# Gated delta stage: the state kept through the update banks by identity products, and the first solved value not copied

## The chip, the cores and the metric

The kernel runs on one core of one Trainium2 chip. The metric is the device time of one execution in microseconds, the median of several runs. The engines are called by their names: TensorE (PE in the profile; PEld is its weight load), VectorE (DVE), ScalarE (ACT), GpSimd (POOL) and SyncE (SP, which issues the DMAs).

## The reference, cut to what matters

The program computes four layers on an activation of 4 x 512 tokens with 128 features; each half layer is followed by a residual sum and a layer norm. The change is in the first of the eight stages, a gated delta rule with 16 heads of 64:

```python
q = silu(dwconv(x @ Wq.T)); k = silu(dwconv(x @ Wk.T)) * 64 ** -0.5; v = silu(dwconv(x @ Wv.T))
a = sigmoid(x @ Wa.T + ba); beta = sigmoid(x @ Wb.T + bb)
def step(S, inp):
    qt, kt, vt, at, bt = inp
    err = einsum('bhij,bhj->bhi', S, kt) - vt
    S = at[..., None] * S - bt[..., None, None] * (err[..., None] * kt[:, :, None, :])
    return S, einsum('bhij,bhj->bhi', S, qt)
S, o = lax.scan(step, S0, xs)          # over the 512 tokens
o = headnorm(o) * ln_w + ln_b; o = o * sigmoid(x @ Wg.T); return o @ Wo.T
```

All arithmetic is in float32. The state S is 64 x 64 for each of 4 x 16 heads, decayed by rows with `a` at each token.

## The kernel before, in words

`delta_attention` (lines 2219 to 2875) cuts the 512 tokens into 16 chunks of 32 (`NC`, `CP`); one pass of the loop works on one chunk n, in two halves e = 0, 1 of 16 tokens, and each half in two blocks u = 0, 1 of 8 tokens. Each engine has its own program, written out by hand; they meet in semaphores, and each engine takes its instructions strictly in order.

In a half, VectorE does this (`one_pass` of the vector block): `steps(n, e, 0)` solves the triangular system of the first 8 tokens, one token after the other, with a product (line 2788) and a sum (2792) for each token over all earlier ones, and a decay of the values so far (2779); `middle` decays what goes over to the second block, decays the state by the whole half (2754, into `ST`) and adds what TensorE computed across the blocks; `steps(n, e, 1)` solves the second block. Its last value releases the transpose into `W` (2784), called the turn in what follows. Then `end` transposes the outputs (2805) and the decays and values of the next chunk into `Y` (2691, 2692), waits for the updates of the state and adds them to the decayed state in four adds of 128x512 (2812), one for each PSUM bank of `UPDATES`. `prepare` (scan at 2697, product at 2700) builds the prefix products of the decays for the next chunk; `norm`, for e = 0 only, is the head norm of the chunk before (2816, 2818); `begin` opens the next half: the transpose of the start products out of PSUM into `Y` (2732) and the inputs of its first block (2722 to 2725). `begin` waits for `laid`, since it overwrites `Y`, from which ScalarE copies, and for `y`, the start products.

TensorE, `boundary(n, e)`: waits for `W`, transposes it in four products with the identity (2437), two for each half of `WT`, waits for ScalarE's copies of them into `WT` (2609), runs 64 small matmuls of 32x64 weights (2448), which put K^T W for the four row groups r into four banks, and then, as each quarter of `ST` is ready, the start products of the next half (2421). Behind that, in its queue, are the projections of the next chunk (2360, 2363), the head norm's sums (`centre` 2463, `variance` 2474), `out` (2482), and for e = 1 the products of the next keys (2374, ahead of the boundary). In e = 0 the boundary stands behind a wait for ScalarE's evacuation of `vN` (line 2555) and in e = 1 behind the products of keys, which wait for the last evacuation of the projections.

ScalarE, around a boundary: the two copies into `WT` (2609), `lay_out` for the next chunk (decays out of `Y` into `aT` 2615, two small copies 2618, 16 copies of values into `bv` 2622, each of them counted by `laid`), `scale_decays` (16 copies into `FB`, 2629, after VectorE's scan), then evacuations.

SyncE's queue holds `spread`: it takes `whole`, from `prepare`, to DRAM and broadcasts it back into `Abc`, which the next decay of the state (2754) reads.

The functions that the diff touches follow.

Of the kernel before, what the change touches and what calls it, by code (L numbers as in the profile page):

```python
# [15 lines left out]
ALU = mybir.AluOpType  # L16
ACT = mybir.ActivationFunctionType
AXX = mybir.AxisListType.X

P = 128  # L20
# [2198 lines left out]
def delta_attention(c):  # L2219
# [17 lines left out]
    GR, GP = 4, NP // 4  # L2237
    UPDATES = (6, 7, 0, 1)
    BEGUN = 7
    GC = 2 * SB * CP + SB  # L2240
# [5 lines left out]
    with ExitStack() as ctx:  # L2246
# [61 lines left out]
        later_ps = ps[:, 4:6, :].rearrange("p h (a n x) -> p h a n x", n=GR, x=XC // 2)  # L2308
        centred_ps = ps[:, 4:6, :].rearrange("p k x -> p (k x)")
        yield []  # L2310
        block = c.block(ctx)
# [38 lines left out]
        def _(eng):  # L2350
# [74 lines left out]
            def boundary(n, e):  # L2425
                j4 = 8 * n + 4 * e

                def next_start(r):
                    eng.wait_ge(s["state"], j4 + max(r + 1, 2 * e))
                    eng.sem_inc(c.past, 1)  # L2430
                    start(1 - e, r)

                eng.wait_ge(s["w"], 4 * n + 2 * e + 2)
                eng.sem_inc(c.past, 1)
                for half in range(2):
                    for g in (2 * half, 2 * half + 1):
                        mm = eng.transpose(ps[:, half, (g % 2) * P:(g % 2 + 1) * P],
                                           W[:, g * GP:(g + 1) * GP, :], c.ident[:, :])
                    mm.then_inc(s["t"], 1)
                eng.wait_ge(s["wc"], 6 * n + 3 * e + 3)  # L2440
                eng.sem_inc(c.past, 1)
                for g in range(GR):
                    for k in range(2):
                        for h in range(2):
                            for r in range(GR):
                                rows, cols = slice(32 * r, 32 * r + 32), slice(DK * h, DK * h + DK)
                                at = (2 * g + k) * DK
                                mm = eng.matmul(ps[cols, UPDATES[r], at:at + DK], KT[rows, e, k, g, cols], WT[rows, g, DK * (h ^ k):DK * (h ^ k) + DK], start=True, stop=True)
                                if (g, k, h) == (GR - 1, 1, 1):
                                    mm.then_inc(s["upd"], 1)  # L2450
                for r in range(GR):
                    next_start(r)
                if e == 1:
                    eng.wait_ge(s["gt"], 2 * n + 3)
                    eng.sem_inc(c.past, 1)
                    later_products(n + 1)
# [82 lines left out]
        def _(eng):  # L2539
# [66 lines left out]
            def boundary(n, e):  # L2606
                for half in range(2):
                    eng.wait_ge(s["t"], 6 * n + 3 * e + half + 2)
                    eng.activation(WT[:, 2 * half:2 * half + 2, :], ps[:, half, 0:2 * P].rearrange("p (g x) -> p g x", x=P), ACT.Copy)\
                       .then_inc(s["wc"], 1)  # L2610

            def lay_out(m, e):
                at = 2 * m + e + 1
                eng.wait_ge(s["transposed"], 3 * at - 2)
                eng.activation(aT[:, e, :, :, 1:].rearrange("p i u t -> p u t i"), decays[:, :, :].rearrange("p (u t) i -> p u t i", t=SB), ACT.Copy)\
                   .then_inc(s["laid"], 1)
                for sign in range(2):
                    eng.activation(beta_now[:, sign, :], half_of(beta, m, e), ACT.Copy, scale=1.0 - 2.0 * sign).then_inc(s["laid"], 1)
                eng.wait_ge(s["transposed"], 3 * at - 1)
                eng.wait_ge(s["laid"], 4 * at - 9)  # L2620
                for t in range(CH):
                    ins = eng.activation(bv[:, e, :, t], values[:, t, :], ACT.Copy, scale=beta_now[:, 0, t:t + 1])
                ins.then_inc(s["laid"], 1)
# [12 lines left out]
            def one_pass(n, first):  # L2636
# [9 lines left out]
                evacuate(n + 1, 2, AV)  # L2646
                boundary(n, 0)
                lay_out(n + 1, 0)
                scale_decays(n + 1, 0)
# [5 lines left out]
                evacuate(n + 1, 6, PROJ)  # L2655
                boundary(n, 1)
                lay_out(n + 1, 1)
                later_products(n + 1)
# [18 lines left out]
        def _(eng):  # L2677
            LINKS = 1 + 3 * SB - 1

# [62 lines left out]
            def middle(n, e):  # L2742
# [8 lines left out]
                eng.tensor_tensor(rest, rest, half[:, e, :].unsqueeze(1).to_broadcast([P, CH, I]), ALU.mult).then_inc(s["begun"], 1)  # L2751
                eng.wait_ge(s["abc"], 2 * 16 * j + 32)
                state = ST[:, :, :].rearrange("p n (s i) -> p n s i", i=I)
                eng.tensor_tensor(state, state, Abc[:, e, :, :, :].rearrange("p s n i -> p n s i"), ALU.mult).then_inc(s["decayed"], 1)
# [7 lines left out]
            def steps(n, e, u):  # L2762
# [12 lines left out]
                settled()  # L2775
                link(eng.tensor_copy(mine[:, :, 0], XP[:, 0, :, SB]))
                for t in range(SB):
                    if t:
                        link(eng.tensor_tensor(mine[:, :, 0:t], mine[:, :, 0:t], aT[:, e, :, u, t + 1].unsqueeze(2).to_broadcast([P, I, t]), ALU.mult))  # L2779
# [6 lines left out]
                    x, keys, seen = 2 * (at + t) + 1, slice(at, at + t + 1), mine[:, :, 0:t + 1]  # L2786
                    if t < SB - 1:
                        link(eng.tensor_tensor(XP[:, :, :, SB - t:], seen.unsqueeze(1).to_broadcast([P, 2, I, t + 1]),  # L2788
                                               G[:, x:x + 2, keys][:, ::-1, :].unsqueeze(2).to_broadcast([P, 2, I, t + 1]), ALU.mult))
                        settled()  # L2790
                        to = first + t + 1
# [9 lines left out]
            def end(n, e, first):  # L2801
                j = 2 * n + e
                if e == 0 and not first:
                    eng.wait_ge(s["centred"], n)
                eng.transpose(O[:, e * CH:(e + 1) * CH, :], OT.rearrange("p i t -> p t i")).then_inc(s["o"], 1)
                turn_values(n + 1, e)
                eng.wait_ge(s["decayed"], j + 1)
                quarters = ST[:, :, :].rearrange("p (g r k) i -> p r g (k i)", r=GR, k=2)
                for r in range(GR):
                    eng.wait_ge(s["upd"], 4 * j + r + 1)  # L2810
                    mine = quarters[:, r, :, :]
                    eng.tensor_tensor(mine, mine, ps[:, UPDATES[r], :].rearrange("p (g x) -> p g x", g=GR), ALU.add).then_inc(s["state"], 1)  # L2812

# [11 lines left out]
            def one_pass(n, first):  # L2825
# [3 lines left out]
                end(n, 0, first)  # L2829
                prepare(n + 1, 0)  # L2830
                if not first:
                    norm(n - 1)
                begin(n, 1)
                steps(n, 1, 0)
# [194 lines left out]
```

## Time and profile before

| | before |
|---|---|
| time, median of 3 runs (lowest, highest) | 2884.49 us (2883.37, 2885.67) |
| the profiled execution's own time | 2877.2 us |
| its span in the trace | 2875.3 us |
| TensorE busy over the span | 2342.6 us (81%) |
| VectorE busy | 2143.5 us (75%) |
| ScalarE busy | 1553.6 us (54%) |
| mean granted TensorE clock | 0.881 of 2.4 GHz |

The span is what the hardware profiler saw from the first to the last instruction. Busy time is the sum over an engine's instructions. A row of the timeline gives the begin and the length of a group of equal instructions in a row, the engine, the line, the operation, what it writes and reads, their number, and in brackets how long the engine stood idle before it and which instruction ended that. Matmuls in float32 appear as two records each. A mean share over the whole span mixes stages: the delta stage is the first 1310 us.

### The profile page before, as it was taken

What the parts mean: (1) busy time and instruction counts of PE and PEld (TensorE: products, weight loads), DVE (VectorE), ACT (ScalarE), POOL (GpSimd) and SP (SyncE); (2) the same over time, 40 slices, a digit from 0 to 9 for tenths busy, and PEclk for the clock granted to TensorE, in tenths of its full rate; (3) what the DMA queues carried; (4) which work ended last, traced back from release to release, by engine and by line L of the source; (5) the groups of instructions that cost most, each with busy time, mean ns of one, the idle gap of its engine ahead of it and who ended that gap; (6) DMA issues with size and microseconds to landing.
All of it is one profiled execution on the core that took longest, in us unless ns stands there. A gap on an engine that the chain in (4) does not pass through costs nothing. (4 is left out here: it accounts for less than half of the span.)

```text
span 2875.3 us, 63093 instructions
## 1 busy us (share of the span) xinstructions
PE 2342.6 (81%) x25365; PEld 1619.3 (56%) x25365; DVE 2143.5 (75%) x4003; ACT 1553.6 (54%) x3983; POOL 264.0 (9%) x278
## 2 busy tenths in 40 slices
PE   6777777777777777777984999999887876999677
PEld 5667667666677667673432666666542322332376
DVE  6999999999999999993123777787626765886465
ACT  3555556666555555655233777777631113667344
POOL 0000000000000000000011101100002431110342
PEclk9888787887887887888996999999998997999888
DMA  5110111110111110102006998899410003221421
GB/s 183 32 31 18 31 31 32 32 32 21 27 31 32 32 31 18 31 17 70 0 11 178 233 250 227 227 248 235 103 37 0 0 0 105 55 82 24 170 70 64
DMA packets 205722, 219.42 MB, mean 76 GB/s; under 512 B 32966, under 2 KB 191446, under 8 KB 199990
## 3 DMA queue, kind: packets, MB, share of 16 engines
q1 hardware_dynamic: 203033, 210.44, 28.1%
q0 software_dynamic: 2400, 4.95, 0.5%
q8 instruction: 203, 3.33, 0.5%
q14 instruction: 86, 0.70, 0.1%
HBM read 137.96 MB, written 79.79 MB: 76 GB/s over the span
## 5 line engine op out<-in xcount | busy, mean ns | idle before, releaser
L2792 DVE TENSOR_REDUCE dl_ZO<-dl_XP 128x64 f32<-128x128 f32 (+6 forms) x448 | 219.8, 491 | 15.4
L2788 DVE TENSOR_TENSOR dl_XP<-dl_ZO,dl_G 128x64 f32<-128x64 f32 (+6 forms) x448 | 194.7, 435 | 15.4
L1973 ACT ACTIVATE da_AB<-ps 128x384 f32<-128x384 f32 x256 | 124.7, 491 | 140.8 <-PE ps L1834 137.2
L2126 DVE TENSOR_TENSOR ps<-ps,da_window 128x192 f32<-128x192 f32 (+1 forms) x256 | 101.3, 396 | 116.8 <-PE ps L1857 112.6
L1453 DVE TENSOR_REDUCE ra_top<-ps 128x1 f32<-128x512 f32 x256 | 159.5, 681 | 36.9 <-PE ps L1219 35.9
L1983 ACT ACTIVATE da_E<-ps,da_top 128x512 f32<-128x512 f32 x256 | 176.2, 688 | 17.5 <-DVE da_top L2129 17.0
L2129 DVE TENSOR_REDUCE da_top<-ps 128x1 f32<-128x512 f32 x256 | 177.0, 691 | 8.8
L1864 PE MATMUL ps<-ident,da_E 128*128 128x128 f32 x1024 | 169.1, 288 | 1.3 <-ACT da_E L1983 1.3
L1353 ACT ACTIVATE ra_PT<-ps 128x512 f32<-128x512 f32 x256 | 136.2, 600 | 61.7 <-PE ps L1250 61.4
L2421 PE MATMUL ps<-dl_kqN,dl_ST 64*64 64x32 f32 x4096 | 114.2, 282 | 42.2 <-DVE dl_ST L2812 36.9
L2363 PE MATMUL ps<-X,dl_taps_q 128*128 128x128 f32 x1088 | 148.3, 304 | 0.0
L2363 PEld LDWEIGHTS ps<-X,dl_taps_q 128*128 128x128 f32 x1088 | 145.2, 219 | 1.8
L1584 POOL MEMSET da_K<- 32x4096 f32 x2 | 7.0, 3505 | 1494.8 <-POOLq L178 1494.7
L2363 PE MATMUL ps<-X,dl_taps_k 128*128 128x128 f32 x1088 | 143.6, 297 | 0.4 <-issue 0.4
L2363 PEld LDWEIGHTS ps<-X,dl_taps_k 128*128 128x128 f32 x1088 | 140.4, 213 | 1.5 <-issue 0.5
L1864 PEld LDWEIGHTS ps<-ident,da_E 128*128 128x128 f32 x1024 | 108.4, 141 | 50.3 <-issue 39.7
L2421 PEld LDWEIGHTS ps<-dl_kqN,dl_ST 64*64 64x64 f32 x4096 | 109.3, 209 | 48.1 <-issue 47.9
L2363 PEld LDWEIGHTS ps<-X,dl_taps_v 128*128 128x128 f32 x1088 | 127.0, 195 | 13.6 <-issue 8.5
L2629 ACT ACTIVATE dl_FB<-dl_F,dl_beta_now 128x32 f32<-128x32 f32 x512 | 126.8, 351 | 9.6 <-DVE dl_F L2697 9.6
L2363 PE MATMUL ps<-X,dl_taps_v 128*128 128x128 f32 x1088 | 127.2, 277 | 4.7 <-DVE dl_taps_v L2853 3.8
L2779 DVE TENSOR_TENSOR dl_ZO<-dl_ZO,dl_aT 128x32 f32<-128x32 f32 (+6 forms) x448 | 128.2, 286 | 0.0
L1219 PE MATMUL ps<-ra_KS,ra_QS 128*128 128x512 bf16 x256 | 104.5, 413 | 12.8 <-DMA ra_KS<-ra_parts 10.2
(404 smaller groups left out, 5726.8 us busy)
## 6 DMA issues: line engine op xcount, KB each, us to landing
da_bands<-da_AB SPq DMA_DIRECT2D x128, 384.0 KB, 3.8
dl_Abc<-dl_ends SPq DMA_DIRECT2D x64, 512.0 KB, 6.3
da_window<-da_bands SPq DMA_DIRECT2D x128, 192.0 KB, 4.4
da_across<-da_bands SPq DMA_DIRECT2D x128, 192.0 KB, 4.5
da_parts<-da_split SPq DMA_DIRECT2D x64, 96.0 KB, 3.4
ra_parts<-ra_split SPq DMA_DIRECT2D x16, 384.0 KB, 3.7
rf_We<-in_rf_We SPq DMA_DIRECT2D x1, 4608.0 KB, 22.9
da_K<-da_parts SPq DMA_DIRECT2D x16, 256.0 KB
```

The lines of the kernel that those rows point to most:

```text
L1353: eng.activation(PT[:, k % 2, h, :], ps[:, tscore_bank(UNITS * m + v), :], ACT.Exp).then_inc(s["exps"], 1)
L1453: eng.tensor_reduce(top[:, m % 2, u:u + 1], ps[:, score_bank(UNITS * m + u), :], AXX, ALU.max, negate=True).then_inc(s["maxima"], 1)
L1864: mm = eng.transpose(ps[:, 2 + U % 2, k * P:(k + 1) * P], E[:, U % 2, k * P:(k + 1) * P], c.ident[:, :])
L1973: eng.activation(AB[:, j % STAGES, h, :, :], ps[:, band_bank(v), 0:2 * BAND].rearrange("p (k x) -> p k x", k=2), ACT.Copy)\
L1983: eng.activation(E[:, U % 2, :], ps[:, score_bank(U), :], ACT.Exp, bias=top[:, u:u + 1], accum_out=total[:, m % 2, u:u + 1]).then_inc(s["e ...
L2129: eng.tensor_reduce(top[:, u:u + 1], bank, AXX, ALU.max, negate=True).then_inc(s["maxima"], 1)
L2363: mm = eng.matmul(out, taps[w][:, tap, cols], columns_of(c.X, m, tap), start=tap == 0, stop=tap == TAPS - 1)
L2421: mm = eng.matmul(starts_ps[e][DK * (h ^ w):DK * (h ^ w) + DK, w, pair // 2, :], ST[rows, pair, :], kqN[rows, pair, e * CH:(e + 1) * CH, : ...
L2629: ins = eng.activation(FB[:, e, :, t // SB, t % SB], F[:, e, :, t // SB, t % SB], ACT.Copy, scale=beta_now[:, 1, t:t + 1])
L2779: link(eng.tensor_tensor(mine[:, :, 0:t], mine[:, :, 0:t], aT[:, e, :, u, t + 1].unsqueeze(2).to_broadcast([P, I, t]), ALU.mult))
L2788: link(eng.tensor_tensor(XP[:, :, :, SB - t:], seen.unsqueeze(1).to_broadcast([P, 2, I, t + 1]), G[:, x:x + 2, keys][:, ::-1, :].unsqueeze ...
L2792: link(eng.tensor_reduce(ZO[:, to:to + 1 + (2 * I - 1) * CH:CH].rearrange("p (k i) -> p k i", k=2), XP[:, :, :, SB - 1 - t:], AXX, ALU.add))
```

## The change

The state is no longer added up on VectorE. TensorE puts the decayed state into the four update banks by a product with the identity for each (`kept`, 512 columns, start=True), the update matmuls add to it there (start=False), and ScalarE copies each bank back into `ST` (`keep_state`), between the copy of the decays and the rest of `lay_out`, which is cut in two for that. `EARLY` says how many of the four identity products stand ahead of the wait for `W`: four for e = 0 and three for e = 1, where the transposes of `W` take bank 1, the fourth update bank; there the fourth identity product and the sixteen updates of r = 3 come last. For e = 0 the transposes of `W` go to banks 2 and 3, for e = 1 both halves to bank 1, so that ScalarE's first copy there waits for both. The next decay of the state on VectorE waits for ScalarE's copies.

In `steps` the first solved value, which was copied out of `XP` and decayed at t = 1, is written already decayed; the product of t = 0 reads it from `XP`, and no decay is issued at t = 1. In `one_pass` of VectorE `norm` and `prepare` of e = 0 change places.

```diff
+    TURNED = ((2, 3), (1, 1))
+    EARLY = (4, 3)
...
+        quarters = ST[:, :, :].rearrange("p (g r k) i -> p r g (k i)", r=GR, k=2)
...
+                def kept(r):
+                    eng.matmul(ps[:, UPDATES[r], :], c.ident[:, :], quarters[:, r, :, :], start=True, stop=False)
+
+                def update(g, k, h, r):
+                    rows, cols = slice(32 * r, 32 * r + 32), slice(DK * h, DK * h + DK)
+                    at = (2 * g + k) * DK
+                    last = (g, k, h) == (GR - 1, 1, 1)
+                    mm = eng.matmul(ps[cols, UPDATES[r], at:at + DK], KT[rows, e, k, g, cols],
+                                    WT[rows, g, DK * (h ^ k):DK * (h ^ k) + DK], start=False, stop=(g, k) == (GR - 1, 1))
+                    if last:
+                        mm.then_inc(s["upd"], 1)
+
+                early = EARLY[e]
+                eng.wait_ge(s["decayed"], 2 * n + e + 1)
+                for r in range(early):
+                    kept(r)
                 eng.wait_ge(s["w"], 4 * n + 2 * e + 2)
...
-                        mm = eng.transpose(ps[:, half, (g % 2) * P:(g % 2 + 1) * P],
-                                           W[:, g * GP:(g + 1) * GP, :], c.ident[:, :])
+                        mm = eng.transpose(ps[:, TURNED[e][half], g * P:(g + 1) * P], W[:, g * GP:(g + 1) * GP, :], c.ident[:, :])
...
-                for g in range(GR):
-                    for k in range(2):
-                        for h in range(2):
-                            for r in range(GR):
...
+                for g, k, h, r in itertools.product(range(GR), range(2), range(2), range(early)):
+                    update(g, k, h, r)
+                for r in range(early, GR):
+                    kept(r)
+                    for g, k, h in itertools.product(range(GR), range(2), range(2)):
+                        update(g, k, h, r)
...
-                    eng.wait_ge(s["t"], 6 * n + 3 * e + half + 2)
+                    eng.wait_ge(s["t"], 6 * n + 3 * e + (3 if e else half + 2))
...
+            def keep_state(n, e):
+                for r in range(GR):
+                    eng.wait_ge(s["upd"], 8 * n + 4 * e + r + 1)
+                    eng.activation(quarters[:, r, :, :], ps[:, UPDATES[r], :].rearrange("p (g x) -> p g x", g=GR), ACT.Copy).then_inc(s["state"], 1)
...
                 boundary(n, 0)
+                lay_decays(n + 1, 0)
+                keep_state(n, 0)
                 lay_out(n + 1, 0)
...
+                if j:
+                    eng.wait_ge(s["state"], 4 * j)
...
-                link(eng.tensor_copy(mine[:, :, 0], XP[:, 0, :, SB]))
+                link(eng.tensor_tensor(mine[:, :, 0], XP[:, 0, :, SB], aT[:, e, :, u, 2], ALU.mult))
                 for t in range(SB):
-                    if t:
+                    if t > 1:
...
+                    if t == 0:
+                        link(eng.tensor_tensor(XP[:, ::-1, :, SB:], XP[:, 0, :, SB:].unsqueeze(1).to_broadcast([P, 2, I, 1]),
+                                               G[:, x:x + 2, keys].unsqueeze(2).to_broadcast([P, 2, I, 1]), ALU.mult))
+                    elif t < SB - 1:
...
-                eng.wait_ge(s["decayed"], j + 1)
-                quarters = ST[:, :, :].rearrange("p (g r k) i -> p r g (k i)", r=GR, k=2)
-                for r in range(GR):
-                    eng.wait_ge(s["upd"], 4 * j + r + 1)
-                    mine = quarters[:, r, :, :]
-                    eng.tensor_tensor(mine, mine, ps[:, UPDATES[r], :].rearrange("p (g x) -> p g x", g=GR), ALU.add).then_inc(s["state"], 1)
...
-                prepare(n + 1, 0)
                 if not first:
                     norm(n - 1)
+                prepare(n + 1, 0)
```

## Rows read from the trace of the kernel before

**Rows 1.** Windows: length, busy time of each engine (instructions), clock, DMA share, GB/s.
```profile
0.00:1310.00 1310.00, 1000.99 (x17026) 895.15 (x17027) 1205.92 (x2381) 761.00 (x2254) 0.20 (x4) 0.83 0.15 36
```

**Rows 2.** Waits of VectorE, 80 to 1300 us: total, times, longest.
```profile
DVE dl_ST L2812 <- PE ps L2448: 25.0, 28, 2.2
```

**Rows 3.** Timeline of VectorE around three boundaries: start, length, engine, line, operation.
```profile
625.03 1.05 DVE L2784 STREAM_TRANSPOSE dl_W<-dl_ZO 128x512 f32<-128x512 f32 x1
628.45 0.67 DVE L2692 STREAM_TRANSPOSE dl_Y<-dl_vN 128x512 f32<-128x512 f32 x1
630.16 2.48 DVE L2812 TENSOR_TENSOR dl_ST<-dl_ST,ps 128x512 f32<-128x512 f32 x4 [1.03 <-PE ps L2448]
...
636.59 1.24 DVE L2732 STREAM_TRANSPOSE dl_Y<-ps 128x1024 f32<-128x1024 f32 x1
...
664.65 1.07 DVE L2784 STREAM_TRANSPOSE dl_W<-dl_ZO 128x512 f32<-128x512 f32 x1
...
669.26 2.48 DVE L2812 TENSOR_TENSOR dl_ST<-dl_ST,ps 128x512 f32<-128x512 f32 x4 [0.51 <-PE ps L2448]
...
676.07 1.25 DVE L2732 STREAM_TRANSPOSE dl_Y<-ps 128x1024 f32<-128x1024 f32 x1
...
704.18 1.05 DVE L2784 STREAM_TRANSPOSE dl_W<-dl_ZO 128x512 f32<-128x512 f32 x1
```

**Rows 4.** Timeline of ScalarE, in the same passes.
```profile
606.06 1.13 ACT L2582 ACTIVATE dl_Q<-ps 128x512 f32<-128x512 f32 x2
...
621.71 1.26 ACT L2555 ACTIVATE dl_vN<-ps,dl_vec 128x128 f32<-128x128 f32 x4 [0.92 <-PE ps L2363]
626.94 0.81 ACT L2609 ACTIVATE dl_WT<-ps 128x256 f32<-128x256 f32 x2 [3.97 <-PE ps L2437]
...
629.51 0.27 ACT L2618 ACTIVATE dl_beta_now<-dl_beta 128x16 f32<-128x16 f32 x2
629.88 3.53 ACT L2622 ACTIVATE dl_bv<-dl_Y,dl_beta_now 128x32 f32<-128x32 f32 x16
...
702.77 1.26 ACT L2555 ACTIVATE dl_vN<-ps,dl_vec 128x128 f32<-128x128 f32 x4 [0.93 <-PE ps L2363]
```

**Rows 5.** Timeline of VectorE, begin of one block of `steps`.
```profile
600.24 0.20 DVE L2776 COPY dl_ZO<-dl_XP 128x32 f32<-128x32 f32 x1
...
600.78 0.30 DVE L2792 TENSOR_REDUCE dl_ZO<-dl_XP 128x64 f32<-128x128 f32 x1
...
601.25 0.31 DVE L2788 TENSOR_TENSOR dl_XP<-dl_ZO,dl_G 128x128 f32<-128x128 f32 x1
```

**Rows 6.** Timeline of TensorE, pieces of several passes.
```profile
190.60 2.10 PE L2374 MATMUL ps<-dl_kqN,dl_kkN 64*64 64x64 f32 x128 [1.45 <-ACT dl_kqN L2555]
193.98 0.63 PE L2437 MATMUL ps<-ident,dl_W 128*128 128x128 f32 x4 [1.29 <-issue]
...
195.23 1.50 PE L2448 MATMUL ps<-dl_WT,dl_KT 32*64 32x64 f32 x118 [0.62 <-ACT dl_WT L2609]
...
236.38 1.84 PE L2448 MATMUL ps<-dl_WT,dl_KT 32*64 32x64 f32 x128 [0.62 <-ACT dl_WT L2609]
...
600.00 1.95 PE L2463 MATMUL ps<-dl_O,dl_sums 128*128 128x512 f32 x4 [0.29 <-ACT dl_GX L2569]
...
601.79 1.95 PE L2467 MATMUL ps<-X,dl_Wg 128*128 128x128 f32 x16
...
611.93 0.68 PE L2407 MATMUL ps<-dl_GX,dl_WT 64*64 64x64 f32 x16
...
627.90 2.18 PE L2448 MATMUL ps<-dl_WT,dl_KT 32*64 32x64 f32 x128 [0.56 <-ACT dl_WT L2609]
...
663.84 2.10 PE L2374 MATMUL ps<-dl_kqN,dl_kkN 64*64 64x64 f32 x128 [1.45 <-ACT dl_kqN L2555]
```

**Rows 7.** Windows of 2 us, columns as in rows 1.
```profile
600.00:602.00 2.00, 2.00 (x6) 1.04 (x7) 1.83 (x8) 2.00 (x10) 0.00 (x0) 1.00 0.15 42
...
628.00:630.00 2.00, 2.00 (x128) 1.94 (x128) 1.12 (x2) 1.34 (x4) 0.00 (x0) 0.53 0.03 8
```

**Rows 8.** Groups by line, delta stage: busy, mean ns, idle before, releaser.
```profile
L2609 ACT ACTIVATE dl_WT<-ps 128x256 f32<-128x256 f32 x64 | 22.6, 383 | 102.5 <-PE ps L2437 101.9
```

More of the change, by code:

```diff
@@ L2441, in boundary @@
                 eng.sem_inc(c.past, 1)
-                for g in range(GR):
-                    for k in range(2):
-                        for h in range(2):
-                            for r in range(GR):
[L2446 to L2450, printed above, removed]
+                for g, k, h, r in itertools.product(range(GR), range(2), range(2), range(early)):
[4 more added lines that the diff above has]
+                        update(g, k, h, r)
                 for r in range(GR):
@@ L2607, in boundary, with lay_decays @@
                 for half in range(2):
-                    eng.wait_ge(s["t"], 6 * n + 3 * e + half + 2)
-                    eng.activation(WT[:, 2 * half:2 * half + 2, :], ps[:, half, 0:2 * P].rearrange("p (g x) -> p g x", x=P), ACT.Copy)\
-                       .then_inc(s["wc"], 1)
-            def lay_out(m, e):
+                    eng.wait_ge(s["t"], 6 * n + 3 * e + (3 if e else half + 2))
+                    eng.activation(WT[:, 2 * half:2 * half + 2, :], ps[:, TURNED[e][half], half * 2 * P:(half + 1) * 2 * P].rearrange("p (g x) -> p g x", x=P),
+                                   ACT.Copy).then_inc(s["wc"], 1)
+            def lay_decays(m, e):
                 at = 2 * m + e + 1
@@ L2616, in lay_out @@
                    .then_inc(s["laid"], 1)
+            def keep_state(n, e):
+                for r in range(GR):
+                    eng.wait_ge(s["upd"], 8 * n + 4 * e + r + 1)
+                    eng.activation(quarters[:, r, :, :], ps[:, UPDATES[r], :].rearrange("p (g x) -> p g x", g=GR), ACT.Copy).then_inc(s["state"], 1)
+            def lay_out(m, e):
+                at = 2 * m + e + 1
                 for sign in range(2):
@@ L2656, in one_pass @@
                 boundary(n, 1)
+                lay_decays(n + 1, 1)
+                keep_state(n, 1)
                 lay_out(n + 1, 1)
@@ L2677, in _ @@
         def _(eng):
-            LINKS = 1 + 3 * SB - 1
+            LINKS = 3 * SB - 1
             def gate_keys(m):
@@ L2786, in steps @@
                     x, keys, seen = 2 * (at + t) + 1, slice(at, at + t + 1), mine[:, :, 0:t + 1]
-                    if t < SB - 1:
+                    if t == 0:
+                        link(eng.tensor_tensor(XP[:, ::-1, :, SB:], XP[:, 0, :, SB:].unsqueeze(1).to_broadcast([P, 2, I, 1]),
+                                               G[:, x:x + 2, keys].unsqueeze(2).to_broadcast([P, 2, I, 1]), ALU.mult))
+                    elif t < SB - 1:
                         link(eng.tensor_tensor(XP[:, :, :, SB - t:], seen.unsqueeze(1).to_broadcast([P, 2, I, t + 1]),
                                                G[:, x:x + 2, keys][:, ::-1, :].unsqueeze(2).to_broadcast([P, 2, I, t + 1]), ALU.mult))
+                    if t < SB - 1:
                         settled()
@@ L2801, in end @@
             def end(n, e, first):
-                j = 2 * n + e
                 if e == 0 and not first:
```

## The prediction, written before the changed kernel was run

> **What bounds the kernel now.** I read the windows first, then the waits of VectorE, then the timelines of VectorE, ScalarE and TensorE around the boundaries between half passes. In the delta stage, which takes the first 1310 us, VectorE is busy 92% of the time and TensorE 76% [rows 1]: VectorE sets the pace. Its waits say where it stops: 25.0 us in 28 stops in front of the state adds of line 2812, [rows 2]; no other wait of it comes near that. So the stage ends when VectorE's queue ends, and what VectorE drops is gained only as far as the next instruction that waits for another engine doesn't come to wait longer. That instruction is the opening transpose of a half pass (line 2732, in `begin`): it overwrites `Y`, and so waits for `laid`, the last of the 16 `bv` copies on ScalarE, and for `y`, the four start products on TensorE. In the trace it waits for neither.
>
> I count time from the turn, the end of the transpose into W (line 2784). In the e = 0 boundary the turn is at 625.03 + 1.05 = 626.08, the state adds begin at 630.16 (+4.08) and the opening transpose at 636.59 (+10.51). In the e = 1 boundary the turn is at 665.72, the adds begin at 669.26 (+3.54), the opening transpose at 676.07 (+10.35) [rows 3]. These two distances are what the change moves. ScalarE has spare time behind its part: the `bv` row ends at 629.88 + 3.53 = 633.41 [rows 4], +7.33, which is 3.2 us before VectorE asks.
>
> **VectorE alone.** Each boundary loses four adds, 2.48 us, and its stop in front of them (630.16 less 628.45 + 0.67 = 1.04 us, [rows 3]). The second edit is in `steps`: the copy becomes a product of the same 32 elements, and the separate product at t = 1 goes. Before, copy to second XP product is 601.25 - 600.24 = 1.01 us. After, the reduce that begins at 600.78 has no product beside it and the XP product waits for its end: 0.54 us from the copy, 0.30 of reduce, 0.04 for the release, 0.88. That is 0.13 us for each of 64 `steps`, not the 0.25 of the deleted row, since it ran under the end of the reduce [rows 5]. Per pass 0.52 us. Norm in front of prepare puts VectorE work ahead of a wait for `aT`, which ScalarE has ready by then; it costs nothing. The transfers of `dl_ends` on SP's queue, which prepare releases, come later by norm's two instructions and sooner by the adds and the stop, 3.5 us, so not later than now.
>
> **TensorE: the 128 identity products are not free.** An identity product of 512 columns is not in the trace, but `centre` has two of that form: they begin at 600.00 and the next row at 601.79, 0.895 us each [rows 6], at a granted clock of 1.00 [rows 7]. Four are 3.6 us, three 2.7 us. They stand in front of the transposes of W in TensorE's queue.
> - e = 0: they can begin only when ScalarE's last evacuation of `vN` is out. That ends at 621.71 + 1.26 = 622.97 (3.11 before its turn) and in the next pass at 704.03, 1.20 before its turn at 705.23 [rows 3, 4]. ScalarE's idle time ahead of the copies of W^T is 101.9 us for 32 boundaries, 3.2 each [rows 8]; in the boundary at 626 it is 3.97 [rows 4], and with the lead of the next pass it would be near 2.2, so the mean lies between the two and I take the middle of them for all. The longest and shortest lead that I find in the 16 passes are 3.7 and 1.0. With 0.14 less from the shorter steps, 0.1 for the release and 3.6 of products, the transposes begin 0.73 and 2.64 after the turn, mean 1.7, in place of 0.27.
> - e = 1: they can begin only behind the products of keys. Those end at 665.94 (0.22 after the turn) and in another pass at 192.70, with the transposes there at 193.98 directly behind its turn, so 1.2 before it [rows 6]. With 2.7 + 0.05 and 0.14 the transposes begin 3.1 and 1.7 after the turn, mean 2.4, in place of 0.14.
>
> **ScalarE: the copies stand ahead of `bv`.** From the begin of the transposes to the begin of the updates is 195.23 - 193.98 = 1.25 us and the 64 updates take 1.84 in the pass at 236 [rows 6]. Then four copies of 128x512 out of PSUM: two of that form (`centre`) take 1.13 us together, 0.57 each [rows 4]; the second begins before the end of the first, so the next in a row adds a little less. I take 0.53, 2.1 us for four. Then beta_now and bv, 629.51 to 633.41, 3.9 us, and 0.1 for the release. So in e = 0 the opening transpose begins 1.25 + 1.8 + 2.1 + 3.9 + 0.1 = 9.1 after the transposes: 1.7 + 9.1 = 10.8, where it was 10.51. All that VectorE lost in adds and stop is eaten: it has its own transposes until 629.12 (+3.0) and then norm and prepare, which today fill 6.43 - 2.4 = 4.0 us between the adds' begin and the opening; so it is ready at +7.1 and waits 3.7 us for `bv`.
> In e = 1 the boundary is longer. Both halves of W^T lie in bank 1, so the first copy waits for both transposes (+0.35). Then 48 updates (1.4), the fourth identity product (0.9), 16 updates of r = 3 alone, its copy (0.53), then 3.9 + 0.1. For the 16 I take 1.36: eight matmuls on two tiles take 0.68 (x16 in the trace, two records for each) [rows 6]. If they ran as in the mixed row, at 1.84 / 64 each, they would take 0.46. Sum 1.6 + 1.4 + 0.9 + 1.36 + 0.53 + 4.0 = 9.8 behind the transposes: 2.4 + 9.8 = 12.2, where it was 10.35. VectorE is ready at 3.0 + (6.81 - 2.4) = +7.4.
> The Trainium skill (TensorE: Matmul & The Clock Gate, Part 3) says that matmuls on different row groups of the array overlap and that packing by columns gives a similar gain. By it, the r = 3 updates alone lose the overlap of the four row groups and keep that of the two column groups; the mixed row of 0.029 us a matmul agrees that packing is at work. The sum is the same with or without this.
>
> Sum for a pass: e = 0 +0.3, e = 1 +1.85, steps -0.52, together +1.6; 16 passes +26 us. The profiled execution took 2877.2 us (span 2875.3, 1.9 around it), so it would take 2903. The median of the three runs is 7.3 us above it, and I carry that: 2884.5 + 26 = 2910.5.
>
> **Bounds.** The identity product: the two of `centre` are 0.895 by their starts and 0.98 by their row's length, and the clock's lower level doubles either; 0.895 is taken because the products of keys just ahead of them take 2.10 us in both passes shown, so no lower clock is seen there. The copies: 0.57 is 5 us above over the stage, 0.49, as far to the other side, 5 below. The r = 3 updates: 0.46 to 1.36, 14 us below. Length of the lead: with the 3.11 lead in all e = 0 boundaries, 15 us below; with 1.20 in all, 15 above. Updates at 2.18 us, as in the row at 627.90, rather than 1.84: 11 above.
>
> **Rivals.**
> 1. The upper clock holds, and everything comes earlier: faster. Today the clock falls after TensorE stands still: it is 0.53 just behind the e = 0 turn, after the stop before it [rows 7]. The identity products fill just that stop. If the clock then stayed up for the projections, `vN` would be out 3.1 before each e = 0 turn and the products of keys 2.6 before each e = 1 turn (the longest leads of more than one pass; the second is that of the pass at 273). Transposes then begin at +0.7 and +0.3, the opening at 9.8 (-0.7) and 10.1 (-0.25), with the steps -1.5 per pass: -24 us, 2860. It decides once both leads exceed 2.5 us; with one of the two, the result is near no change (about 2885). For it: the low clock is seen after stops. Against: the stops that slow the projections, in front of the middle of each half, stay as they are.
> The Trainium skill (same page, Part 1) has it that lack of activity throttles the array and activity releases it. The 0.53 agrees with that for this kernel. The rule alone would make this rival the forecast; what speaks against it is that the products fill a different stop from those ahead of the projections.
> 2. VectorE alone counts: the adds, 79 us in 32 boundaries, the stops, 25, and the steps, 8, come off: 2772. For it: 92% busy. Against: the wait for `laid` has only 3.2 us of cover, and the copies, 2.1, and the later transposes use it up.
> 3. The identity products run at the lower clock in half of the boundaries: 3 us more in each, +50 on top of the forecast: 2960. For it: the clock is low in parts of every pass. Against: the products of keys, just ahead of those of e = 1, take the same 2.10 us in both passes [rows 6].
>
> **How the numbers follow.** The forecast has 0.60, rival 1 0.25 (0.17 for the full one, 0.08 for near no change), rival 2 0.06, rival 3 0.09. 0.2% is 5.8 us, about what a measurement of this kernel can tell from no change. Faster 0.23, same 0.08, slower 0.69. The range goes from rival 1, with something to spare, 2855, to 2950, where the longer updates and a part of the lower clock add to the forecast.
>
> **What would show it.** In the changed trace: the opening transpose in `begin` waits for ScalarE's `bv` rows, about 3 us, 32 times; VectorE's busy time in the stage is down by some 90 us and its idle time up by more; the identity products take 0.9 us each, and the transposes of W begin 1.7 us (e = 0) and 2.4 us (e = 1) after the turn; from there to the opening transpose 9.1 and 9.8 us; VectorE is nowhere else later. I am wrong if the opening transpose doesn't wait, if the leads in front of the identity products come out longer than today's, or if a pass is under 78 us.

## The result, and the profile after

| | before | after |
|---|---|---|
| time, median (lowest, highest) | 2883.93 us (2881.21, 2885.67), 4 runs | 2913.06 us (2907.53, 2917.85), 4 runs |
| ratio to before, 95% interval | 1 | 1.0109 (1.0083 to 1.0135) |
| the profiled execution's own time, span | 2877.2, 2875.3 us | 2917.85, 2916.0 us |
| VectorE busy over the span | 2143.5 us | 2060.7 us |
| ScalarE busy | 1553.6 us | 1614.5 us |
| TensorE busy | 2342.6 us | 2407.9 us |

The change makes the kernel 1.1% slower, 29 us by the medians; 2910.5 was forecast. The four runs after fall into two pairs, 2907.5 and 2908.4, 2917.8 and 2917.9; the profiled execution is of the upper pair, and that of the kernel before was 7 us below its median, so the differences in the traces add up to some 40 us and not 29. By the ratio, which the experiments are compared with, the change costs 31 us (24 to 39).

The windows of the whole delta stage, from 80 us to just before its last turn, columns as in [rows 1], first before, then after:

```profile
80.00:1292.00 1212.00, 940.00 (x16152) 841.07 (x16152) 1137.85 (x2275) 720.74 (x2143) 0.00 (x0) 0.82 0.13 28
```

```profile
80.00:1330.00 1250.00, 996.49 (x16336) 828.36 (x16338) 1058.14 (x2090) 780.55 (x2267) 0.00 (x0) 0.90 0.12 27
```

VectorE has 80 us less to do and the stretch is 38 us longer: its idle time went from 74 to 192 us. The waits of VectorE say where. The one of [rows 2] is gone, and these stand in its place (line 2759 is the opening transpose, 2645 the `bv` copies, 2785 the transpose of the cross products):

```profile
DVE dl_Y L2759 <- ACT dl_bv L2645: 130.9, 30, 6.1
DVE dl_D L2785 <- PE ps L2410: 6.5, 16, 0.5
DVE dl_Y L2759 <- PE ps L2424: 6.0, 1, 6.0
```

One boundary of e = 0 and one of e = 1 in the trace after. VectorE (2813 is the transpose into W, whose end is the turn), as in [rows 3]:

```profile
766.28 1.07 DVE L2813 STREAM_TRANSPOSE dl_W<-dl_ZO 128x512 f32<-128x512 f32 x1
...
774.55 0.22 DVE L2727 TENSOR_TENSOR dl_whole<-dl_F 128x32 f32<-128x32 f32 x1
779.54 1.25 DVE L2759 STREAM_TRANSPOSE dl_Y<-ps 128x1024 f32<-128x1024 f32 x1 [4.77 <-ACT dl_bv L2645]
...
806.95 1.06 DVE L2813 STREAM_TRANSPOSE dl_W<-dl_ZO 128x512 f32<-128x512 f32 x1
...
815.08 0.22 DVE L2727 TENSOR_TENSOR dl_whole<-dl_F 128x32 f32<-128x32 f32 x1
820.24 1.25 DVE L2759 STREAM_TRANSPOSE dl_Y<-ps 128x1024 f32<-128x1024 f32 x1 [4.94 <-ACT dl_bv L2645]
```

TensorE, as in [rows 6]: 2437 are the identity products, 2456 the transposes of W, 2443 the updates.

```profile
765.49 2.10 PE L2377 MATMUL ps<-dl_kqN,dl_kkN 64*64 64x64 f32 x128 [1.45 <-ACT dl_kqN L2570]
767.51 2.84 PE L2437 MATMUL ps<-dl_ST,ident 128*128 128x512 f32 x6
770.19 0.60 PE L2456 MATMUL ps<-ident,dl_W 128*128 128x128 f32 x4
771.63 1.28 PE L2443 MATMUL ps<-dl_WT,dl_KT 32*64 32x64 f32 x96 [0.84 <-ACT dl_WT L2624]
772.84 1.13 PE L2437 MATMUL ps<-dl_ST,ident 128*128 128x512 f32 x2
773.89 1.15 PE L2443 MATMUL ps<-dl_WT,dl_KT 32*64 32x64 f32 x32
...
807.99 3.70 PE L2437 MATMUL ps<-dl_ST,ident 128*128 128x512 f32 x8 [1.35 <-ACT dl_vN L2570]
811.53 0.60 PE L2456 MATMUL ps<-ident,dl_W 128*128 128x128 f32 x4
812.75 1.58 PE L2443 MATMUL ps<-dl_WT,dl_KT 32*64 32x64 f32 x128 [0.62 <-ACT dl_WT L2624]
```

ScalarE, as in [rows 4]: 2636 are the state copies, 2645 `bv`.

```profile
772.89 1.57 ACT L2636 ACTIVATE dl_ST<-ps 128x512 f32<-128x512 f32 x3 [0.36 <-PE ps L2443]
775.09 0.60 ACT L2636 ACTIVATE dl_ST<-ps 128x512 f32<-128x512 f32 x1 [0.62 <-PE ps L2443]
775.58 0.31 ACT L2641 ACTIVATE dl_beta_now<-dl_beta 128x16 f32<-128x16 f32 x2
775.98 3.53 ACT L2645 ACTIVATE dl_bv<-dl_Y,dl_beta_now 128x32 f32<-128x32 f32 x16
...
814.32 2.06 ACT L2636 ACTIVATE dl_ST<-ps 128x512 f32<-128x512 f32 x4 [0.67 <-PE ps L2443]
...
816.68 3.53 ACT L2645 ACTIVATE dl_bv<-dl_Y,dl_beta_now 128x32 f32<-128x32 f32 x16
```

To be seen: in e = 1 (turn at 767.35) the three identity products keep the transposes of W until +2.8; `bv` ends at 779.51 and the opening follows 0.03 later, at +12.2. VectorE had finished with prepare at 774.77, +7.4. In e = 0 (turn at 808.01) four products end where the transposes begin, +3.5, and the opening is at +12.2. Over all 16 passes of the trace the means are, in us after the turn (the forecast's first row is the mean of the two passes that it used):

| | before, e = 0 | after, e = 0 | forecast | before, e = 1 | after, e = 1 | forecast |
|---|---|---|---|---|---|---|
| last evacuation of vN (e = 0), end of the keys' products (e = 1) | -2.0 | -1.0 | -2.2 | -0.4 | -0.2 | -0.5 |
| transposes of W begin | 0.25 | 2.6 | 1.7 | 0.14 | 2.4 | 2.4 |
| updates end | 4.2 | 5.4 | | 3.5 | 7.45 | |
| opening transpose | 10.4 | 11.3 | 10.8 | 10.3 | 12.0 | 12.2 |

### The profile page after: what moved, and what is told of

The parts are those of the page before. It is cut to its first block and busy times, and to the rows that moved or that the text cites. A ratio compares the mean times of both kernels' runs of the same rounds, so it can differ in the third digit from the quotient of the medians.

```text
span 2916.0 us, 63556 instructions
## 1 busy us (share of the span) xinstructions
PE 2407.9 (83%) x25621; PEld 1612.0 (55%) x25621; DVE 2060.7 (71%) x3811; ACT 1614.5 (55%) x4111; POOL 263.8 (9%) x278
## 5 line engine op out<-in xcount | busy, mean ns | idle before, releaser
L2820 DVE TENSOR_TENSOR dl_XP<-dl_ZO,dl_G 128x128 f32<-128x128 f32 (+5 forms) x384 | 177.0, 461 | 13.2
L2437 PE MATMUL ps<-dl_ST,ident 128*128 128x512 f32 x256 | 122.7, 612 | 21.5 <-ACT dl_vN L2570 21.5
L2759 DVE STREAM_TRANSPOSE dl_Y<-ps 128x1024 f32<-128x1024 f32 x32 | 40.0, 1250 | 141.5 <-ACT dl_bv L2645 135.5
L2366 PE MATMUL ps<-X,dl_taps_k 128*128 128x128 f32 x1088 | 129.8, 279 | 0.3 <-issue 0.3
L2366 PEld LDWEIGHTS ps<-X,dl_taps_k 128*128 128x128 f32 x1088 | 126.4, 195 | 1.3 <-issue 0.5
L1219 PE MATMUL ps<-ra_KS,ra_QS 128*128 128x512 bf16 x256 | 104.5, 413 | 13.0 <-DMA ra_KS<-ra_parts 10.3
L2808 DVE TENSOR_TENSOR dl_ZO<-dl_ZO,dl_aT 128x64 f32<-128x64 f32 (+5 forms) x384 | 114.8, 299 | 0.0
```

The source lines that it names most:

```text
L2366: mm = eng.matmul(out, taps[w][:, tap, cols], columns_of(c.X, m, tap), start=tap == 0, stop=tap == TAPS - 1)
L2437: eng.matmul(ps[:, UPDATES[r], :], c.ident[:, :], quarters[:, r, :, :], start=True, stop=False)
```

## The experiments

All are compared with the kernel before on the same chip; "than after" uses the difference of the ratios to it, times 2884 us, and is good to some 10 us.

### 1. The edit in `steps` alone

The kernel before, with

```diff
-                link(eng.tensor_copy(mine[:, :, 0], XP[:, 0, :, SB]))
+                link(eng.tensor_tensor(mine[:, :, 0], XP[:, 0, :, SB], aT[:, e, :, u, 2], ALU.mult))
...
-                    if t:
+                    if t > 1:
```

and the product of t = 0 as in the change.

> The kernel before with the edit in `steps` alone (first solved value written decayed, no copy and no product at t = 1); the state is added on VectorE as before. My reading: the deleted product ran under the end of the reduce, so 64 x 0.13 = 8 us less than before, about 2876. Rival (the deleted row counts in full): 64 x 0.25 = 16 us less, 2868. In the trace the distance from the first product of a block to its second XP product falls from 1.01 to 0.88 us.

Measured: 2871.11 us, ratio 0.9964 (0.9952 to 0.9975), so 10 us less (7 to 14). The 8 us hold, and the 16 are outside. In the traces, from the first product of a block to its second XP product it is 0.90 us in the mean of the 64 blocks and was 1.00, and from an opening to the next turn 28.53 us and was 28.75.

### 2. Half of the `bv` copies

```diff
-                for t in range(CH):
+                for t in range(0, CH, 2):
                     ins = eng.activation(bv[:, e, :, t], values[:, t, :], ACT.Copy, scale=beta_now[:, 0, t:t + 1])
```

> The changed kernel with only every second of the 16 `bv` copies issued (half of the `bv` copies are left out), so ScalarE has 1.77 us less between the state copies and the release of `Y`. My theory (the opening transpose waits for ScalarE's queue): each opening comes 1.77 us sooner, in 32 boundaries 56 us less than the changed kernel, about 2857, and the start products of TensorE are then almost the next bound. Rival (TensorE's products are late and hold it by `y`, or VectorE itself is the bound): 0 to 10 us less.

Measured: 2852.59 us, ratio 0.9898 (0.9875 to 0.9922), 61 us less than after. ScalarE's queue ahead of the release of `Y` is what the opening waits for: 8 copies take 1.83 us in that trace in place of 3.53. That 61 is so near to 56 is in part chance. In that trace the transposes of W also begin earlier than after, by 0.7 us (e = 0) and 0.4 us (e = 1) in the mean, and in four boundaries the opening waits for the start products instead:

```profile
DVE dl_Y L2759 <- ACT dl_bv L2645: 55.7, 27, 3.6
DVE dl_Y L2759 <- PE ps L2424: 17.0, 4, 5.0
```

### 3. Without the identity products

```diff
-                for r in range(early):
-                    kept(r)
...
-                                    WT[rows, g, DK * (h ^ k):DK * (h ^ k) + DK], start=False, stop=(g, k) == (GR - 1, 1))
+                                    WT[rows, g, DK * (h ^ k):DK * (h ^ k) + DK], start=True, stop=True)
...
                 for r in range(early, GR):
-                    kept(r)
```

> The changed kernel without the identity products (the decayed state is left out of the sum; the updates start their banks), all else as it is. My theory: the transposes of W begin at once after the turn, 2.4 us sooner in both boundaries, and in e = 1 the fourth product's 0.9 us goes too; 16 x (2.4 + 2.3 + 0.9) = about 85 to 90 us less than the changed kernel, 2825, which would be 58 us below the kernel before. Rival (ScalarE's copies alone are the cost, the products are hidden): within 10 us of the changed kernel.

Measured: 2851.85 us, ratio 0.9897 (0.9874 to 0.992), 61 us less than after. The rival is out, the products do stand on the path; but they are worth 61 us and not 85 to 90. The boundaries of this trace show two reasons. ScalarE in one of e = 1 (turn at 656.20), then TensorE in one of e = 0, then the clock there:

```profile
658.68 1.16 ACT L2627 ACTIVATE dl_aT<-dl_Y 128x512 f32<-128x512 f32 x1 [0.74 <-DVE dl_Y L2715]
659.63 2.09 ACT L2633 ACTIVATE dl_ST<-ps 128x512 f32<-128x512 f32 x4
661.60 0.33 ACT L2638 ACTIVATE dl_beta_now<-dl_beta 128x16 f32<-128x16 f32 x2
662.02 3.53 ACT L2642 ACTIVATE dl_bv<-dl_Y,dl_beta_now 128x32 f32<-128x32 f32 x16
```

```profile
617.94 1.08 PE L2454 MATMUL ps<-ident,dl_W 128*128 128x128 f32 x4 [2.93 <-DVE dl_W L2810]
619.59 2.25 PE L2443 MATMUL ps<-dl_WT,dl_KT 32*64 32x64 f32 x128 [0.56 <-ACT dl_WT L2621]
```

```profile
618.00:620.00 2.00, 1.44 (x33) 1.06 (x37) 1.97 (x3) 0.77 (x2) 0.00 (x0) 0.50 0.01 4
620.00:622.00 2.00, 1.84 (x121) 1.65 (x108) 1.96 (x4) 1.34 (x2) 0.00 (x0) 0.50 0.03 8
```

First, there is a floor that I had not in the sum: the decays are in `Y` at +2.5, and `aT` (0.95), four copies (2.0), two small ones and `bv` (3.9) follow without a gap, so in this order of ScalarE's queue the opening cannot come before +9.4, however early TensorE is. In the mean of the 16 passes it comes at +9.5 in e = 1 and at +9.9 in e = 0. Second, without the identity products the clock is at its lower level again in the e = 0 boundary, and transposes and updates take 1.08 and 2.25 us where the changed kernel has 0.60 and 1.58 (the clock there is 1.00):

```profile
812.00:814.00 2.00, 1.38 (x119) 1.28 (x122) 1.82 (x3) 1.65 (x3) 0.00 (x0) 1.00 0.00 0
```

The stage as a whole, without the identity products, has the clock of the kernel before, 0.83:

```profile
80.00:1270.00 1190.00, 943.87 (x16156) 848.87 (x16156) 1058.74 (x2093) 782.59 (x2268) 0.00 (x0) 0.83 0.13 29
```

This version is 30 us below the kernel before, 10 of them for the `steps` edit if its worth is the same here: free of the identity products, the state copies on ScalarE are only some 20 us better than the adds on VectorE.

### 4. The identity products of banks 6 and 7 earlier

```diff
-                eng.wait_ge(s["decayed"], 2 * n + e + 1)
-                for r in range(early):
-                    kept(r)
+                for r in range(2, early):
+                    kept(n, e, r)
...
                 project(n + 1, 2, AV, False)
-                eng.wait_ge(s["evac"], (n + 1) * PROJ + AV)
                 if not first:
                     eng.wait_ge(s["log"], 2 * n - 1)
+                kept(n, 0, 0)
+                kept(n, 0, 1)
+                eng.wait_ge(s["evac"], (n + 1) * PROJ + AV)
                 boundary(n, 0)
...
-                products_of_keys(n + 1)
                 if not first:
                     eng.wait_ge(s["wo_copied"], n)
+                kept(n, 1, 0)
+                kept(n, 1, 1)
+                products_of_keys(n + 1)
                 boundary(n, 1)
```

`kept` is `kept(n, e, r)` here and waits for `decayed` itself at r = 0.

> The changed kernel with the identity products of banks 6 and 7 moved ahead in TensorE's queue: for e = 0 ahead of the wait for the last evacuation of vN, for e = 1 ahead of the products of keys, where TensorE stands still 1.35 and 1.45 us. My theory: the transposes of W begin 1.3 us (e = 0) and 1.45 us (e = 1) sooner, 16 x 2.75 = 44 us less than the changed kernel, about 2869, below the kernel before. Rival (the lead isn't what counts): no change, 2913.

Measured: 2861.81 us, ratio 0.9929 (0.9906 to 0.9952), 52 us less than after, where 44 were expected; only the place of two of the four products in the queue is another. In the trace of e = 1 two of them now run before the products of keys, and only one stands right ahead of the transposes (two in e = 0). The transposes begin at +0.9 (e = 0) and +0.8 (e = 1) in the mean, 1.8 and 1.6 us sooner than after:

```profile
654.80 1.88 PE L2431 MATMUL ps<-dl_ST,ident 128*128 128x512 f32 x4
656.61 2.10 PE L2377 MATMUL ps<-dl_kqN,dl_kkN 64*64 64x64 f32 x128
658.63 1.12 PE L2431 MATMUL ps<-dl_ST,ident 128*128 128x512 f32 x2
659.60 0.60 PE L2457 MATMUL ps<-ident,dl_W 128*128 128x128 f32 x4
```

### 5. The early products of e = 1 twice

```diff
-                def kept(r):
+                def kept(r, twice=False):
+                    if twice:
+                        eng.matmul(ps[:, UPDATES[r], :], c.ident[:, :], quarters[:, r, :, :], start=True, stop=True)
...
-                    kept(r)
+                    kept(r, e == 1)
```

> The changed kernel with the three early identity products of e = 1 issued twice each (the first result is overwritten by the second), 48 products more. My theory (the products ahead of the transposes of W stand on the path at 0.9 us each): 16 x 2.7 = 43 us more than the changed kernel, about 2956, less some where the products of keys end early. Rival (they lie in TensorE's idle time): within 10 us of the changed kernel.

Measured: 2954.18 us, ratio 1.0258 (1.0232 to 1.0285), 43 us more than after (32 to 54), as expected. The six begin 0.86 us apart in that trace (the first two 0.96), and the transposes of W begin at +4.7 in the mean of e = 1, where they began at +2.4. The two traces differ by 35 us.

### 6. No move to other engines: the adds later

```diff
+            def add_state(n, e):
...
                 end(n, 0, first)
-                prepare(n + 1, 0)
                 if not first:
                     norm(n - 1)
+                add_state(n, 0)
+                prepare(n + 1, 0)
...
                     residual(n - 1)
+                add_state(n, 1)
                 prepare(n + 1, 1)
```

Besides, it has the edits of experiment 1; norm goes ahead of prepare here too.

> The kernel before with the edit in `steps`, and on VectorE the four state adds moved behind norm (e = 0) and behind the transpose of the keys' products and the residual (e = 1); nothing goes to TensorE or ScalarE. My theory: the stops of 25 us in front of the adds are filled with that work, the start products still end before the opening transpose; 25 + 10 us less than the kernel before, about 2847. Rival (the start products come later and the opening waits for them): at most the 10 us of the `steps` edit, 2871 or more.

Measured: 2882.07 us, ratio 1.0012 (1.0001 to 1.0022). My expectation failed: the 25.0 us of stops in front of the adds are gone, but 30.5 us stand in front of the opening, now by the start products, and the run is 14 us above experiment 1. The waits, one e = 1 boundary on VectorE and TensorE (2818 the adds, 2421 the start products), and the clock there:

```profile
DVE dl_Y L2732 <- PE ps L2421: 30.5, 30, 1.9
```

```profile
671.76 2.47 DVE L2818 TENSOR_TENSOR dl_ST<-dl_ST,ps 128x512 f32<-128x512 f32 x4
...
676.95 1.25 DVE L2732 STREAM_TRANSPOSE dl_Y<-ps 128x1024 f32<-128x1024 f32 x1 [1.20 <-PE ps L2421]
```

```profile
673.18 3.64 PE L2421 MATMUL ps<-dl_kqN,dl_ST 64*64 64x32 f32 x128 [3.63 <-DVE dl_ST L2818]
```

```profile
672.00:674.00 2.00, 0.82 (x32) 0.85 (x34) 2.00 (x4) 1.27 (x6) 0.00 (x0) 0.50 0.00 0
```

I had taken 0.8 us from the last add to the end of the start products, as in the pass at 626; here it is 2.6. But 0.8 is the shortest of the 32 in the trace before: there it is 2.0 in the mean of e = 0 and 2.8 in that of e = 1, and this run has 2.2 and 2.7. The start products of the boundary at 665.72 before, and the clock there:

```profile
670.70 3.56 PE L2421 MATMUL ps<-dl_kqN,dl_ST 64*64 64x32 f32 x128 [1.49 <-DVE dl_ST L2812]
```

```profile
672.00:674.00 2.00, 2.00 (x86) 2.00 (x80) 1.97 (x1) 1.04 (x5) 0.00 (x0) 0.50 0.03 8
```

So they ran as slowly there, and the longer stop of TensorE in this run has not slowed them. Before, they ended at +8.6 and +8.8, only 1.8 and 1.5 us ahead of the opening. The adds of e = 1 now begin at +5.8, 2.4 us later, more than that cover, and the opening comes at +11.1 where it came at +10.3; in e = 0, 1.2 us later, it is at +10.0 for +10.4.

### 7. Shared copies

From experiment 4: ScalarE copies the banks of r = 0 and 1, VectorE those of r = 2 and 3, with a semaphore of its own.

```diff
             def keep_state(n, e):
-                for r in range(GR):
+                for r in range(2):
...
+            def keep_rest(n, e):
+                for r in range(2, GR):
+                    eng.wait_ge(s["upd"], 8 * n + 4 * e + r + 1)
+                    eng.tensor_copy(quarters[:, r, :, :], ps[:, UPDATES[r], :].rearrange("p (g x) -> p g x", g=GR)).then_inc(s["state_v"], 1)
```

Left out here: the calls of `keep_rest` ahead of prepare, and the waits of the start products and of the next decay for the two semaphores.

> The kernel of the run before with the identity products moved ahead, and of the four state copies ScalarE makes those of r = 0 and 1 and VectorE those of r = 2 and 3, behind norm (e = 0) or the residual (e = 1), where it stands waiting for `bv`. My theory: ScalarE's queue ahead of `bv` is 1.05 us shorter in e = 0 and 1.6 us in e = 1, 16 x 2.65 = 42 us less than 2862, about 2820. Rival (VectorE is the bound as soon as it takes work back): 2.4 us more work on it per pass and at most 10 us less.

Measured: 2838.75 us, ratio 0.9859 (0.9842 to 0.9875); the same kernel again, on the chip of experiment 10:

> The kernel with shared copies, two and two, once more, beside its neighbour with three and one on the same chip. As measured the first time: 2839, ratio to the kernel before 0.986.

2853.88 us, ratio 0.9853 (0.9836 to 0.9871), on a chip whose runs of the kernel before were at 2894. It is 20 us less than experiment 4, more than the rival allowed and half of what I expected. In the trace the opening is at +8.8 in both boundaries, where experiment 4 has +9.7 and +10.3. It waits little now, the cross products (line 2795) are waited for more (11.7 us, 4.6 in experiment 4), and VectorE is the bound again:

```profile
DVE dl_D L2795 <- PE ps L2410: 11.7, 13, 2.1
DVE dl_Y L2768 <- ACT dl_bv L2654: 9.9, 15, 2.1
DVE dl_Y L2768 <- PE ps L2424: 4.8, 6, 1.4
```

This version beats both kernels: 1.4% below the kernel before.

### 8. Norm behind prepare again

```diff
+                prepare(n + 1, 0)
                 if not first:
                     norm(n - 1)
-                prepare(n + 1, 0)
```

> The changed kernel with norm behind prepare again in e = 0. My theory: no change (within 5 us of the changed kernel, 2913), since VectorE waits for `bv` behind both; it stops for `aT` in front of prepare instead. Rival (the order of the two is worth the 2.6 us of norm): up to 40 us more.

Measured: 2904.39 us, ratio 1.0091 (1.0072 to 1.0111). No gain from the new order is seen; the 5 us in favour of the old one lie within the intervals. VectorE does stop for `aT`, 22.0 us in 17 stops, and waits 109.8 us for `bv` in place of 130.9.

### 9. The rest of the change, with the old `steps`

The changed kernel with the two edits of experiment 1 taken back.

> The changed kernel with `steps` as in the kernel before (copy, and the product at t = 1); the rest of the change stays. My theory: the two parts add, so the changed kernel's time plus the 10 us that the `steps` edit alone was worth, 2921. Rival (the shorter steps only bring the turn nearer to the late identity products, so they are worth nothing for the second block of a half): plus 5 us, 2916.

Measured: 2922.53 us where the kernel before had 2894.14, ratio 1.0101 (1.0081 to 1.0121). The 2922.53 meets the number of the expectation only because this chip's times are 10 us higher for every kernel; the ratio decides. If the two parts added, the ratio would be 1.0109 + 0.0036 = 1.0145, outside the interval; with the intervals of all three counted the gap is 13 us, give or take 10. Within the change the `steps` edit is worth nothing that shows (-2 us, give or take 10).

### 10. Three copies on ScalarE, one on VectorE

As experiment 7, with `range(3)` and `range(3, GR)`.

> The kernel with shared copies, with three state copies on ScalarE (r = 0 to 2) and one on VectorE (r = 3), in place of two and two. My theory: ScalarE's queue ahead of `bv` is 0.53 us longer and is again what the opening waits for; 32 x 0.5 = 16 us more than with two and two, about 2855. Rival (VectorE is the bound with two and two): 0.6 us less on VectorE in each boundary, up to 19 us less.

Measured: 2868.17 us, ratio 0.9903 (0.9883 to 0.9924), beside 2853.88 for two and two on the same chip: 14 us more, 16 were expected. The opening waits for `bv` again:

```profile
DVE dl_Y L2768 <- ACT dl_bv L2654: 39.3, 28, 3.6
```

## Why the prediction was right

The time, the sign and the way were as forecast, and experiments 2, 4, 5 and 10 each move one term by about its price; experiment 3 has two thirds of it. By the steps of the prediction:

- **The bound moves to the wait for `laid`.** Right: 130.9 us in 30 stops, and 61 us less for 56 us less of `bv` (experiment 2). A stop is 4.4 us in the mean; the prediction's list has about 3, its own sums have 3.7 and 4.8.
- **The identity products on the path, 0.9 us each.** Right: eight records in 3.70 us against 3.6 forecast, and 43 us for 48 more of them (experiment 5). What I had not in the sum is that they pay part of it back: they fill a part of TensorE's stop in front of the e = 0 turn, and the clock is not at its lower level behind it. Rival 1 is half true: the stage's clock rose from 0.82 to 0.90, updates take 1.58 us in each of the 16 boundaries of e = 0, not 1.84 (and 1.84 was one pass's: before, 13 of the 16 have 2.24 or 2.25), and experiment 3 shows the lower clock there again without the products. It wasn't enough to turn the sign, for the reason given: the projections were not earlier.
- **The lead in e = 0.** Mis-sized by 1.2 us. I took the mean of two passes, 2.2, unchanged; the trace before has 2.0 over its 16 passes, the profiled execution after has 1.0. The lead goes with the clock under the products ahead of it. In both traces the two products of `variance` take 1.98 us where the lead is 2.5 or more, and 2.7 to 3.8 where it is shorter; it is 1.98 in five of the 15 passes before that have it, and in three after. From their begin to the end of the projections of V it is 9.9 us in the mean before and 10.5 after, and they begin 0.4 us later against the turn. In the pass at 808, the shortest lead (0.07), the granted clock is 0.50 from 794 to 798 us, under `variance`; in the pass at 626 before, with 3.1, it is 1.00 from 610 us on. The lead isn't a fixed property: it is 1.6 and 1.9 in the profiles of experiments 8 and 9, whose TensorE and ScalarE programs are the same, and their stages are 11 and 12 us shorter. The two pairs of times after, 10 us apart, would fit this, but no profile of the lower pair shows it.
- **From the transposes of W to the opening.** 9.1 and 9.8 us forecast, 8.7 and 9.6 measured. The four copies took 2.06 (2.1), the 16 updates of r = 3 1.15 (1.36), the 64 of e = 0 1.58 (1.84). The errors here are to the other side than the lead's, and in the sum they take back two thirds of it. The 1.58 came by the clock, which I had not counted on: that is luck.
- **`steps`.** The size was right for the edit alone (8 forecast, 10 measured), and in the trace after from the first product to the second XP product it is 824.00 - 823.10 = 0.90 us against 0.88 forecast:

```profile
823.10 0.22 DVE L2805 TENSOR_TENSOR dl_ZO<-dl_XP,dl_aT 128x32 f32<-128x32 f32 x1
823.35 0.27 DVE L2817 TENSOR_TENSOR dl_XP<-dl_XP,dl_G 128x64 f32<-128x64 f32 x1
823.66 0.30 DVE L2825 TENSOR_REDUCE dl_ZO<-dl_XP 128x64 f32<-128x128 f32 x1
824.00 0.31 DVE L2820 TENSOR_TENSOR dl_XP<-dl_ZO,dl_G 128x128 f32<-128x128 f32 x1
```

  But as a term of the whole, -0.52 us per pass was wrong. From one opening to the next turn the trace has 28.70 us where it had 28.75. The edit itself shortens this stretch as much as it does alone: 28.91 to 28.70 within the change (experiment 9's trace and this one), 28.75 to 28.53 without it (experiment 1). The rest of the change lengthens it by 0.16. Most of that is the wait for the cross products (line 2785), 6.5 us in all where it was 2.6; it is 6.3 with the old `steps` too, so it isn't the edit that brings it. And a turn that comes sooner finds the identity products as late as ever. I charged that second effect to the leads but counted the whole gain all the same. Experiment 9 shows nothing left by the times; which part of that is this effect, and which the lead that moves from run to run, is open.
- **Norm ahead of prepare.** Nothing, as forecast (experiment 8).
- **VectorE's 90 us less.** It is 80 us in the stage, 83 over the span; all of it, and 38 us more, is waiting now.

So against the trace, which has 38 us more from the first turn of the stage to its last, the sum of +26 is 12 too low: 15 for the begin of the transposes in e = 0 (2.6 for 1.7) and 7 for the stretch from opening to turn, less 10 for that from the transposes to the opening. Against the medians it is 3 too low, and against the ratio 5, because the execution profiled before was 7 us below its median and the one after 5 above; that the forecast and the medians agree so closely is partly luck. Rival 2 is out by 141 us. Rival 3 is out too: none of the 256 records of the identity products is longer than 0.70 us, where those of `variance`, of the same size, reach 1.22 at the lower clock.

```profile
L2437 PE MATMUL ps<-dl_ST,ident x256: 592/592/697, 78.9 to 1336.9; 128*128 128x512 f32 x128
L2489 PE MATMUL ps<-dl_Q,dl_sums x64: 592/1061/1220, 147.2 to 1355.2; 128*128 128x512 f32 x64
```

## What to carry to other kernels

Work taken off the busiest engine is worth only the cover of the next wait behind it: list what the next instruction on that engine waits for and how long each of those has been ready (here 3.2 us for `bv`, but only 1.5 to 1.8 for the start products), and charge the moved work to the queues that feed it. On an engine with a strict order the place of an added instruction can count more than the instruction: two of four products moved a few instructions ahead, to where the engine stood still anyway, turned +31 us into -20. A price read from one pass can be the odd one out: 0.8 us for the end of the start products was, and experiment 6 failed by it. And once copies can go to either of two engines, split them so that both arrive together; two and two gave -1.4%, three and one -1.0%.

## What the runs showed of the hardware

Added matmuls can make their neighbours faster. With the identity products in TensorE's stop the granted clock of the stage was 0.90, without them 0.83 (experiment 3) and 0.82 (before), and the same 64 updates took 1.58 us in place of 2.25. The gain was smaller than the price of the products themselves, 0.9 us each, as long as these stood in front of the transposes (+31 us); with two of four moved ahead the kernel was 20 us below the one before. The clock of a stage also says little of one stretch in it: while the mean rose, `variance` and the projections of V took 0.6 us more.
